# First FFN of a macaron block: the second expert's rounding on ScalarE, and two splits moved on VectorE

## What is computed

```python
def ffn(x, ...):                      # mixture of experts, 2 of 8 per batch row
    logits = x.reshape(b, -1) @ switch_w.T + switch_b
    gate, top_idx = top_k(softmax(logits), 2)
    h = gelu(xh @ w1[top_idx] + b1[top_idx])      # 16 heads of 32 features
    o = (gate * (h @ w2[top_idx] + b2[top_idx])).sum(experts)
    return (x + o) @ w3.T + b3

x = x + 0.5 * ffn(layernorm(x))
x = x + attention(layernorm(x))       # w_in: 5 projections, a gated scan, w_out
x = x + 0.5 * ffn(layernorm(x))
```

## Time and profile before

| | |
|---|---|
| median of 3 runs | 590.75 us (589.7 to 591.27) |
| the profiled execution, its own time | 590.24 us |
| its span, first to last instruction | 588.5 us |
| TensorE (PE) busy, over the span | 517.6 us, 88% |
| VectorE (DVE) busy | 427.7 us, 73% |
| ScalarE (ACT) busy | 219.4 us, 37% |
| GpSimd (POOL) busy | 136.6 us, 23% |
| mean granted TensorE clock | 0.974 of full speed |

### The profile page before, as it was taken

One profiled execution on the slowest core, in us unless ns is written; L12 is line 12 of the kernel. 1 busy time (PEld: TensorE's weight loads), 2 busy tenths in 40 slices (PEclk: granted clock), 3 DMA queues, 4 the chain that ended last, 5 costly groups with the idle time before them and its releaser, 6 DMA issues.

```text
span 588.5 us, 7982 instructions
## 1 busy us (share of the span) xinstructions
PE 517.6 (88%) x2837; PEld 373.0 (63%) x2860; DVE 427.7 (73%) x796; ACT 219.4 (37%) x367; POOL 136.6 (23%) x132
## 2 busy tenths in 40 slices
PE   0594899999899999989999999999999746799997
PEld 0482576666576666758666666766667744577776
DVE  3758887997975777796477798735886777997752
ACT  0126635323615233261433344233330027666540
POOL 3140012454001224401322420122330101321220
PEclk9886999999999999999999999999999897999999
DMA  8995004000002000010200001030118940013012
GB/s 286 368 411 240 1 0 162 1 1 1 36 19 88 3 0 2 1 37 19 89 0 0 0 0 53 0 125 1 55 53 323 383 152 2 4 51 126 36 55 89
DMA packets 16608, 48.15 MB, mean 82 GB/s; under 512 B 1600, under 2 KB 1856, under 8 KB 15296
## 3 DMA queue, kind: packets, MB, share of 16 engines
q1 hardware_dynamic: 15760, 47.19, 21.3%
q10 hardware_dynamic: 816, 0.54, 0.4%
HBM read 39.33 MB, written 8.39 MB: 81 GB/s over the span
## 4 chain that ended last, share of the span: by engine, by line
PE 58%; DVE 15%; issue 14%; POOL 6%; DMA 4%; ACT 2%; SPq 0%; DVEq 0%; POOLq 0%
PE bank L386 9%; PE bank L388 8%; PE bank L387 8%; PE bank L683 7%; PE bank L688 7%; PE bank L684 7%; DMA route_w<-in_switch_w 4%; POOL rs L1054 4%; PE bank L490 3%; DVE h_lo L1250 2%; DVE h_hi L1249 2%; PE bank L518 2%; POOL rs_wide L1059 1%; PE bank L594 1%; PE bank L536 1%
## 5 line engine op out<-in xcount | busy, mean ns | idle before, releaser
L683 PE MATMUL bank<-xh,win_hi 128*128 128x512 f32 x300 | 133.7, 446 | 0.0
L684 PE MATMUL bank<-xl,win_hi 128*128 128x512 f32 x300 | 118.1, 394 | 0.0
L688 PE MATMUL bank<-xbf,win_lo 128*128 128x512 bf16 x289 | 80.1, 381 | 1.5
L1054 POOL TENSOR_TENSOR rs<-ms,neg_half 128x16 f32<-128x16 f32 x16 | 49.8, 3114 | 130.2 <-ACT ms L897 130.2
L683 PEld LDWEIGHTS bank<-xh,win_hi 128*128 128x128 f32 x300 | 56.4, 188 | 21.0 <-issue 3.2
L684 PEld LDWEIGHTS bank<-xl,win_hi 128*128 128x128 f32 x300 | 56.5, 188 | 11.1
L1041 POOL TENSOR_TENSOR xa<-xa,b_half 128x512 f32<-128x512 f32 x28 | 40.6, 1461 | 64.5 <-DVE z_lo L1268 32.1
L386 PE MATMUL bank<-w_hi,z_hi 128*128 128x512 f32 x128 | 51.6, 403 | 0.0
L388 PE MATMUL bank<-w_hi,z_lo 128*128 128x512 f32 x128 | 50.1, 391 | 0.0
L387 PE MATMUL bank<-w_lo,z_hi 128*128 128x512 f32 x128 | 49.9, 390 | 0.0
L834 ACT ACTIVATE hf<-bank,w_sel 128x512 f32<-128x512 f32 x64 | 41.9, 687 | 20.0 <-DVE h_lo L1250 9.6
(11 more groups left out here) (185 smaller groups left out, 1044.9 us busy)
## 6 DMA issues: line engine op xcount, KB each, us to landing
route_w<-in_switch_w SPq DMA_DIRECT2D x4, 2048.0 KB, 14.0
route_w<-in_switch_w SPq DMA_DIRECT2D x16, 512.0 KB, 16.3
raw<-in_w_in SPq DMA_DIRECT2D x4, 1280.0 KB, 19.1
xa<-in_x SPq DMA_DIRECT2D x4, 1024.0 KB, 6.4
out<-x SPq DMA_DIRECT2D x16, 256.0 KB, 2.0
x_dram<-x1p SPq DMA_DIRECT2D x12, 256.0 KB, 2.0
xa<-x_dram SPq DMA_DIRECT2D x3, 1024.0 KB, 5.6
x_chunk<-in_x SPq DMA_DIRECT2D x2, 1024.0 KB, 23.3
```

The costliest lines, as they stand in the source:

```text
L683: pe.matmul(bank[:], win_hi[:, c, r, k, :], xh[:, k, :], start=(k == 0), stop=False)
L684: pe.matmul(bank[:], win_hi[:, c, r, k, :], xl[:, k, :], start=False, stop=False)
L688: mm = pe.matmul(bank[:], win_lo[:, c, r, k, :], xbf[:, k, :], start=False, stop=(k == KC - 1))
L1054: pool.tensor_tensor(rs[:], ms[:], neg_half[:], ALU.pow).then_inc(s_rs, 1)
```

## The change

ScalarE gets a new step, second_hi, behind each gelu(0, c): it rounds hf[:, 1] into h_hi[:, 1] and adds to s_hh. For chunk 0 it waits for the selection of w2, for the others for O(c - 1). VectorE's split_hidden, for f = 0 and k = 1, waits for that instead of rounding itself; k = 0 is as before. The waits for s_hh in the late FFNs count four more. On VectorE w3_lo is made behind the last split_hidden and ahead of z_split(0, 2), and split_in(0) stands behind the whole of w3_norm(0, 0).

```diff
--- before.py
+++ after.py
@@ -843,6 +843,16 @@
                     act.wait_ge(s_gelu, H_JOBS * f + TOPK * c + k + 1)
                     act.activation(hi[:, k, :], src[:, k, :], ACT.Copy).then_inc(s_hh, 1)
 
+            def second_hi(f, c):
+
+                src, hi, _ = hid_set(f, c)
+                if c == 0:
+                    act.wait_ge(s_sel[1], f + 1)
+                else:
+                    act.wait_ge(s_ob, job_ffn(f, f"O{c - 1}") + 1)
+                act.wait_ge(s_gelu, H_JOBS * f + TOPK * c + TOPK)
+                act.activation(hi[:, 1, :], src[:, 1, :], ACT.Copy).then_inc(s_hh, 1)
+
             def z_out(f, c):
                 act.wait_ge(s_ob, job_ffn(f, f"O{c}") + 1)
                 use = ffn_set(f)
@@ -939,11 +949,14 @@
                 load_table(ACT.Gelu)
                 split_in(0)
                 gelu(0, 0)
+                second_hi(0, 0)
                 gelu(0, 1)
+                second_hi(0, 1)
                 for c in range(KC):
                     z_out(0, c)
                     if c < 2:
                         gelu(0, c + 2)
+                        second_hi(0, c + 2)
 
             table_loads()
             for t in range(1, NT):
@@ -1246,13 +1259,16 @@
                     ve.wait_ge(s_gelu, H_JOBS * f + TOPK * c + k + 1)
                     if k == 0 and read_job is not None:
                         ve.wait_ge(s_ob, read_job + 1)
-                    own.do(ve.tensor_copy(hi[:, k, :], src[:, k, :]))
+                    if k == 1 and isinstance(f, int) and f == 0:
+                        ve.wait_ge(s_hh, c + 1)
+                    else:
+                        own.do(ve.tensor_copy(hi[:, k, :], src[:, k, :]))
                     ve.tensor_tensor(lo[:, k, :], src[:, k, :], hi[:, k, :], ALU.subtract).then_inc(s_hl, 1)
 
             def hidden_lo(f, c):
                 src, hi, lo = hid_set(f, c)
                 for k in range(TOPK):
-                    ve.wait_ge(s_hh, H_JOBS * (f - B) + TOPK * c + k + 1)
+                    ve.wait_ge(s_hh, H_JOBS * (f - B) + TOPK * c + KC + k + 1)
                     ve.tensor_tensor(lo[:, k, :], src[:, k, :], hi[:, k, :], ALU.subtract).then_inc(s_hl, 1)
 
             def xt_split(f, c):
@@ -1372,18 +1388,20 @@
             by_half(0)
             select(0, 0, 1, lambda: gate(0))
             split_hidden(0, 0, None)
-            ve.wait_ge(s_w3h, 1)
-            ve.scalar_tensor_tensor(out=w3_lo[:], in0=w3_raw[:], scalar=0.5, in1=w3_hi[:], op0=ALU.mult,
-                                    op1=ALU.subtract).then_inc(s_w3l, 1)
             for c in range(KC):
                 job = job_first(f"O{c}")
                 if c < KC - 1:
                     split_hidden(0, c + 1, job)
+                if c == KC - 2:
+                    ve.wait_ge(s_w3h, 1)
+                    ve.scalar_tensor_tensor(out=w3_lo[:], in0=w3_raw[:], scalar=0.5, in1=w3_hi[:], op0=ALU.mult,
+                                            op1=ALU.subtract).then_inc(s_w3l, 1)
                 z_split(0, c, x_bank[c])
-            split_in(0)
             for t in range(NT):
                 job = job_first(f"W{t}")
                 w3_norm(0, t, job, out_bank(f"W{t}"))
+                if t == 0:
+                    split_in(0)
             split_in(1)
             split_in(2)
             own.do(ve.memset(starts[:], 0.0))
```

## The result

The changed kernel takes 592.33 us in the median (591.48 to 593.03, 8 runs), against 590.78 us (589.70 to 591.27, 8 runs) for the kernel before on the same chip: a ratio of 1.0027, 95% interval 1.0017 to 1.0037, or 1.6 us more (1.0 to 2.2). The forecast was 592.0, 1.2 us more than before.

What follows compares the result with a forecast made beforehand. The prediction took TensorE to bound the stretch, VectorE 0.1 us behind. W0's -0.28 and the split's +1.51 gave +1.23 us: 590.24 becomes 591.5 profiled, plus 0.5 to the median, 592.0 us; range 590.2 to 593.7.

Steps and rivals of the forecast that it cites:

- The step: First FFN, one chunk's step: 2.97 us instead of 3.33, bound by TensorE, with ScalarE's rounding hidden.
- rival (b): First FFN steps: the rounding on ScalarE wins nothing, steps grow back towards 3.33 us, slower, 593.2 us; chance 0.07.
- w3_lo: Moved behind the last low part: TensorE waits 1.1 us for it, W0 starts at 67.90, a gain of only 0.28 us.
- The split: split_in(0) behind W0 on VectorE: 2.73 us, delays norm1 of block 0, TensorE stands 1.5 us; counted as +1.51 us.
- the sum of +1.23: Whole stretch: -0.28 us for W0 and +1.51 us for the split's place.
- Rival (c): Transpose ahead of W3: late norm1 doesn't hold TensorE, only W0's gain of -0.28 us stays, 590.5 us; chance 0.10.
- (d): Ahead of W0: more of the step gain gets through, at best -0.6 us, 590.2 us; chance 0.03.
- rival (a): TensorE's two new waits: its clock falls to half for some 3 us, 1.6 us more, 593.6 us; chance 0.08.
- start-to-start times: VectorE handovers: successors start 0.08 us before the predecessor's end; the skill's rule instead would give W0 0.16 us later, 592.1.
- Equal distances after that: Sign of being right: behind the w_in products, 1.2 us later than before, distances equal those of the kernel before.
- A fifth of 0.72: Chances: the forecast has 0.72, a fifth of it may show over 1.8 us slower; slower was given 0.26.
- GpSimd's rstd works between VectorE's steps as before: Ahead of norm1 of block 0: claimed GpSimd's rstd still works between VectorE's steps; no size given.

Runs made afterwards that it cites:

- e8: e1 plus 21 matmuls without use on TensorE ahead of hidden(0, 0): 589.52 us, ratio 0.9979 to the kernel before.
- e5: The kernel before with w3_lo's move alone, VectorE rounding both experts: 592.23 us, ratio 1.0022 to the kernel before.
- e6: The kernel before with split_in(0)'s move alone, VectorE rounding both experts: 592.29 us, ratio 1.0018 to the kernel before.
- e7: The changed kernel with the moved split made by two VectorE instructions of half the columns: 592.16 us, ratio 1.0024 to the kernel before.
- e2: The changed kernel with split_in(0) put back ahead of the W tiles: 590.64 us, ratio 0.9994 to the kernel before.
- e3: The changed kernel with w3_lo put back behind the first split_hidden: 591.32 us, ratio 1.0006 to the kernel before.
- e1: The changed kernel with both VectorE moves undone, only the rounding on ScalarE left: 589.70 us, ratio 0.9982 to the kernel before.
- e4: The changed kernel without second_hi: both moves kept, VectorE rounding both experts: 593.78 us, ratio 1.0044 to the kernel before.
- e9: e8 plus w3_lo in halves, one at the old place, one behind the last split_hidden: 589.96 us, ratio 0.9989 to the kernel before.
- e10: e9 plus 26 matmuls without use ahead of hidden(4, 0) in the second FFN: 589.44 us, ratio 0.9987 to the kernel before.

## Why the prediction was right

*The step.* 2.97 us was forecast, and 2.97 measured. ScalarE's rounding takes 0.632 to 0.637 us each of the four times and no one waits for it: rival (b) falls. *w3_lo.* TensorE's idle time ahead of W0 was forecast as 1.1 us and is 1.2. W0 starts 0.12 us earlier from the origin (23.91 against 24.03), where 0.28 was forecast: O0 ended 0.09 us later than in the trace before, because the clock rose later (0.72 from 57 to 58, against 0.91), and the first W matmul follows w3_lo's end by 0.10 instead of 0.04. *The split.* The tile's work of 1.81 us and the split's 2.73 are there to the digit (71.36, 73.17, 75.90). norm1 is 1.38 us later from the origin, the w_in product 1.38: the sum of +1.23 was 0.15 short, all of it W0's start. Rival (c) falls with the 1.3 us wait of L594, and (d) with the gap ahead of W0. The medians give 1.6 us with an interval that holds 1.4 and the forecast 1.2. The prediction held that 1.2 us can't be told from no change; with eight runs of each kernel the interval leaves no change out.

*The clock*, rival (a): both new waits, 1.2 and 1.3 us, left the granted clock at 1.00.

```profile
66.00:68.00 2.00, 1.08 (x5) 0.56 (x3) 2.00 (x1) 0.88 (x2) 0.00 (x0) 1.00 0.00 0
...
76.00:78.00 2.00, 0.70 (x4) 0.23 (x2) 1.91 (x4) 0.00 (x0) 0.40 (x1) 1.00 0.00 0
```

It falls. The Trainium skill, TensorE: Matmul & The Clock Gate, section "HAM oscillation — how this bites in real kernels", tells of a kernel whose short bursts stand between longer waits for DMA and which is throttled each time. The two new waits here (1.2 and 1.3 us) stand alone in denser work, and the clock stayed at 1.00; e8's fall at 54.7, after bursts between waits of 1.8 and 1.3 us, is of the kind that the section describes, at still shorter waits than its own. The Trainium skill's section "The DRAIN you can't avoid" (VectorE: DVE Perf Modes) has the next operation start when the pipe is empty, and adds that one which isn't held starts earlier. The prediction took only the first half of this. Here z_lo starts at 59.93, 0.08 us ahead of the low parts' end at 60.01, so the start-to-start times that the prediction added up were the right ones.

*Behind the stretch.* "Equal distances after that" did not come in the profiled execution: from the first w_in matmul to the end of the span it took 507.7 us, against 506.5 before. It isn't the change's doing: e5 and e6, with one move each and no rounding, have 507.7 too, and e7, the whole change with its split in two, 506.8.

*A sum that was off.* A fifth of 0.72, with 0.08 and 0.07 for (a) and (b), gives 0.29 for slower and not 0.26. It touches neither the forecast nor the range.

*A step that was wrong without harm:* "GpSimd's rstd works between VectorE's steps as before". It works beside the split and takes 3.07 us. It ends at 76.40, 0.95 us ahead of norm1; had norm1 stood right behind the split, at 75.90, it would have had to wait for it (argued from the rows, not run).

*The whole as a design.* The rounding wins 1.5 us in this stretch; each move gives that back: w3_lo by TensorE's wait ahead of W0 (e2), the split by norm1 (e3); both together give back 2.9 (after against e1: 39.26 and 36.38). The lowest ratios of all have e8 (0.9979) and e1 (0.9982), which their intervals don't tell apart; e1 is the simpler kernel.

## What to carry to other kernels

In this kernel, moving work out of a visible wait was worth only what the next deadline left: write down, for each place in the queue, who is next behind it and when the bound engine asks for that. When two edits aim at the same stall, time them apart: here one of them was enough and the other two cost more than it won. VectorE's idle gap ahead of W0's end was free for the split (e1); right behind W0's end the same split cost 1.4 us (e6).

## What the runs showed of the hardware

- A GpSimd operation of 0.56 us on one column, started beside a VectorE subtraction of 2.81 us with two inputs in SBUF, took 3.07 us; with that subtraction in halves, 1.74 us. It took 3.07 us in all four kernels with the split in one piece behind W0 (after, e3, e4, e6). It ends about 0.4 us after the VectorE instruction that it met, each time. Beside a VectorE addition with one input in PSUM (e1, 75.34 to 76.03) the same operation took 0.56:

```profile
75.39 0.56 POOL L1059 TENSOR_TENSOR rstd<-mv,neg_half 128x1 f32<-128x1 f32 x1 [1.65 <-DVE mv L1316]
```

The Trainium skill, Advanced Engine Details and Errata, section "GPSIMD Details", says that the two engines share an interface and conflict at VectorE instructions with two SBUF inputs; 3.07 against 0.56 us agrees.
- Most of the scatter of this kernel's runs goes with the clock. In one set of 33 runs of the kernel before, the 15 with a mean granted clock of 0.965 to 0.968 took 590.64 to 591.10 us, and the 8 with 0.977 or 0.980 took 589.48 to 589.72. Not all of it does: on another chip one of 23 runs took 593.50 at 0.968, where the others at 0.965 to 0.968 took 590.85 to 591.95. The changed kernel's eight go from 593.03 at 0.967 to 591.48 at 0.977. Where its profiled execution lost 1.2 us more behind the stretch, the clock was at 0.50 from 468 to 474 (before: 0.82) and 0.57 from 484 to 500 (before: 0.68). That these periods are the whole of the 1.2 us was not tried.
- Filling an idle stretch of TensorE did not keep its clock up for what came after. The 21 matmuls end at 49.2 in e8; the clock fell among the sparse matmuls behind them, at about 54.7 in e8, 54.4 in e9 and already 52.0 in e10, and the next dense ones, O0, ran at 1.2 GHz. e9 and e10 have the same code up to there, so the moment of the fall varies between executions by over 2 us.
